# Attention interleaved with a recurrence: a third x buffer, spaced recurrence steps, and two transpositions of each group in scores banks

## What is computed

```python
qkv = x @ c_attn_w + c_attn_b                      # 16 heads of 32
k = concat([cond @ uk_w.T + uk_b, k_word]); v = concat([cond @ uv_w.T + uv_b, v_word])
scores = q @ k.T / sqrt(32), causal (the condition's key is seen by all), + mask
x1 = x + softmax(scores) @ v @ c_proj_w + c_proj_b
h = cond; for t in range(512): h = tanh(h @ Wh + x1[:, t] @ Wx + b)    # 8 rows at once
out = x1 + all h
```

## Time and profile before

| | us |
|---|---|
| median of 3 runs | 1680.48 |
| lowest, highest | 1677.81, 1688.58 |
| profiled execution, its own time | 1685.94 |
| its span from the first to the last instruction | 1684.2 |

### The profile page before, as it was taken

One profiled execution on the slowest core, in us unless ns is written; L12 is line 12 of the kernel. 1 busy time (PEld: TensorE's weight loads), 2 busy tenths in 40 slices (PEclk: granted clock), 3 DMA queues, 4 the chain that ended last, 5 costly groups with the idle time before them and its releaser, 6 DMA issues.

```text
span 1684.2 us, 74145 instructions
## 1 busy us (share of the span) xinstructions
PE 1543.0 (92%) x32749; PEld 1231.0 (73%) x32749; DVE 778.1 (46%) x2687; ACT 667.5 (40%) x2257; POOL 184.5 (11%) x300
## 2 busy tenths in 40 slices
PE   6889989999999999999999999999999989998775
PEld 5667767777777777777777777777778767777554
DVE  4445343544444444544545454454554544565221
ACT  3434333344343433444334443344444434444111
POOL 2112111111110101111010110100101101100000
PEclk8869999999999999999999999999999999999999
DMA  6323121212222222333323232323232432421000
GB/s 229 94 51 86 42 64 49 75 44 75 61 79 78 72 61 71 81 81 86 84 73 91 80 99 83 92 82 96 82 93 70 134 85 70 127 91 42 16 9 15
DMA packets 167903, 130.24 MB, mean 77 GB/s; under 512 B 54264, under 2 KB 153112, under 8 KB 167072
## 3 DMA queue, kind: packets, MB, share of 16 engines
q1 hardware_dynamic: 153792, 92.92, 19.4%
q0 software_dynamic: 13792, 32.58, 6.8%
HBM read 100.00 MB, written 25.43 MB: 74 GB/s over the span
## 4 chain that ended last, share of the span: by engine, by line
PE 81%; DVE 5%; issue 4%; ACT 4%; DMA 3%; SPq 2%; POOL 0%; DVEq 0%; ACTq 0%; POOLq 0%
PE rec L1053 26%; PE dense L983 9%; PE dense L499 9%; PE dense L501 7%; PE dense L500 7%; PE rec L1044 7%; PE scores L975 5%; PE pv L1000 4%; PE pv L1018 2%; PE scores L1053 2%; DMA xin<-x 2%; DVE pre L879 2%; ACT states L732 1%; SPq L524 1%; PE dense L1011 1%
## 5 line engine op out<-in xcount | busy, mean ns | idle before, releaser
L1053 PE MATMUL rec<-wh,states 128*32 128x128 f32 x15360 | 517.7, 275 | 33.6 <-ACT states L732 32.5
L1053 PEld LDWEIGHTS rec<-wh,states 128*32 128x32 f32 x15360 | 401.0, 110 | 119.1 <-ACT states L732 60.3
L879 DVE STREAM_TRANSPOSE pre<-rec 128x128 f32<-128x128 f32 x480 | 152.0, 317 | 515.4 <-PE rec L1053 514.7
L732 ACT ACTIVATE states<-pre 128x32 f32<-128x32 f32 x512 | 133.8, 261 | 510.8 <-DVE pre L879 510.1
L683 ACT ACTIVATE probs<-probs,nmax 128x64 f32<-128x64 f32 (+7 forms) x512 | 271.2, 531 | 103.8 <-DVE nmax L823 100.8
L983 PE MATMUL dense<-ident,probs 128*128 128x128 f32 (+1 forms) x1252 | 229.1, 290 | 31.3 <-DVE probsT L833 8.4
L823 DVE CUSTOM_DVE_ANT_0 probs<-scores,msk,nimg 128x64 f32<-128x64 f32 (+7 forms) x512 | 245.8, 501 | 13.3 <-PE scores L975 6.1
L983 PEld LDWEIGHTS dense<-ident,probs 128*128 128x128 f32 (+1 forms) x1252 | 129.4, 135 | 96.4 <-issue 58.4
L499 PE MATMUL dense<-xT_hi,wqkv_hi 128*128 128x256 f32 x504 | 155.4, 308 | 13.8 <-DVE nimg L809 6.7
L691 ACT COPY probsT<-dense 128x256 f32<-128x256 f32 (+4 forms) x248 | 104.6, 422 | 112.2 <-PE dense L983 111.8
L833 DVE COPY probsT<-dense 128x256 f32<-128x256 f32 (+4 forms) x236 | 119.1, 504 | 59.5 <-PE dense L983 54.7
(11 more groups left out here) (138 smaller groups left out, 1751.4 us busy)
## 6 DMA issues: line engine op xcount, KB each, us to landing
vbuf<-v_dram SPq DMA_DIRECT2D x64, 192.0 KB, 2.8
xin<-x SPq DMA_DIRECT2D x64, 128.0 KB, 2.8
v_dram<-vbuf POOLq DMA_DIRECT2D x64, 128.0 KB, 2.8
out<-outs POOLq DMA_DIRECT2D x32, 256.0 KB, 4.6
vbuf<-v_dram SPq DMA_DIRECT2D x64, 128.0 KB, 2.4
kt<-k_dram SPq DMA_DIRECT2D x16, 512.0 KB, 5.1
vbuf<-v_dram SPq DMA_DIRECT2D x32, 256.0 KB, 3.2
k_dram<-knew POOLq DMA_DIRECT2D x60, 128.0 KB, 2.6
```

The costliest lines, as they stand in the source:

```text
L732: act.activation(state_cells(g), pre[:].rearrange("p f (b z) -> p f b z", z=GROUP)[:, :, :, s], ACT.Tanh).then_inc(h_ready, 1)
L879: dve.transpose(pre_all, rec_bank(g // GROUP)[:, 0:P]).then_inc(pre_ready, 1)
L1053: last = pe.matmul(rec_bank(g // GROUP)[Q * j:Q * j + Q, 0:P], state_tile(g - 1)[:, f, :], wh[:, f, P * j:P * j + P], start=False, stop=f ...
```

## The change

- x has three buffers (XTILES); `xload` of trips 1 and 2 is issued at the start, and `finish(g)` loads trip g + 3 instead of g + 2. SBUF for it comes from the key ring: ROOM goes from 3 to 2 tiles of the longest kind.
- `xsplit` of the next trip goes from head 15 or 16 to 11, and its chunks begin at head 13 instead of 16 or 18.
- In `order`, a step is placed only when at least PACE = 0.7 of weight has been emitted since the step before it.
- The turns of heads with u % 4 in (1, 2) go to `scores[1]` and `scores[2]`, outside the rotation. Such a turn waits for `shifted_ready` of head g + 4, the head whose scores stand in that bank by then; the scores that take the bank next wait for the copy of that turn.
- The `softmax` events of a group are emitted two at the group's first head and one at each of the next two, instead of one, two and one.

```diff
-ROOM = 3 * 2 * S
+ROOM = 2 * 2 * S
-SPLIT_AT = (16, 16, 15, 15, 15, 15, 15, 15)
-CHUNK_AT = (18, 18, 16, 16, 16, 16, 16, 16)
+SPLIT_AT = (11, 11, 11, 11, 11, 11, 11, 11)
+CHUNK_AT = (13, 13, 13, 13, 13, 13, 13, 13)
+XTILES = 3
+PACE = 0.7
...
-        return ([("proj", g, c, 1.5) for c in range(C)] + [("xload", g + 2, 0, 0.0)] * (g + 2 < TRIPS)
+        return ([("proj", g, c, 1.5) for c in range(C)] + [("xload", g + XTILES, 0, 0.0)] * (g + XTILES < TRIPS)
...
-         + chunk(0, 0) + [("vimg", 0, 0, 3.7)] + chunk(0, 1) + chunk(0, 2) + [("xload", 1, 0, 0.0)])
+         + chunk(0, 0) + [("vimg", 0, 0, 3.7)] + chunk(0, 1) + chunk(0, 2) + [("xload", 1, 0, 0.0), ("xload", 2, 0, 0.0)])
...
-            emit([("softmax", v, 0, 0.0) for v in ((u,), (u, u + 1), (u + 1,), ())[u % HC]])
+            emit([("softmax", v, 0, 0.0) for v in ((u, u + 1), (u + 1,), (u + 1,), ())[u % HC]])
...
-    done, t = 0.0, 0
+    done, t, step_at = 0.0, 0, 0.0
...
-               and (done >= whole * (t + 0.5) / FIRST or at + 1 == last)):
+               and (done >= max(whole * (t + 0.5) / FIRST, step_at + PACE) or at + 1 == last)):
             place.setdefault(at, []).append(t)
-            t += 1
+            t, step_at = t + 1, done
...
-        if kind in DENSE_KINDS + ("turn",) and kind != "v":
+        if kind == "turn" and g % HC in (1, 2):
+            n = 2 + g % HC
+            JOB[kind, g, i] = n, uses[n]
+            uses[n] += 1
+        elif kind in DENSE_KINDS + ("turn",) and kind != "v":
...
-        xin = sb("xin", [P, 2, PAIRED, C, P])
+        xin = sb("xin", [P, XTILES, PAIRED, C, P])
...
-        banks = dense + [rec]
+        banks = dense + [rec] + scores[1:3]
...
-                    if g > 1:
-                        wait_copied(sp, "proj", g - 2, C - 2)
-                        wait_copied(sp, "proj", g - 2, C - 1)
+                    if g >= XTILES:
+                        wait_copied(sp, "proj", g - XTILES, C - 2)
+                        wait_copied(sp, "proj", g - XTILES, C - 1)
...
                     if g >= HC:
                         pe.wait_ge(shifted_ready, g - HC + 1)
+                    if j in (1, 2) and group > 1:
+
+                        wait_copied(pe, "turn", g - 2 * HC, 0)
...
                     pe.wait_ge(probs_ready, g + 1)
-                    wait_bank(pe, kind, g, 0)
+                    if g % HC in (1, 2):
+
+                        pe.wait_ge(shifted_ready, min(g + HC + 1, HEADS))
+                    else:
+                        wait_bank(pe, kind, g, 0)
```

More of the change, by code:

```diff
@@ L266, in attention_recurrence @@
     ORDER = order()
-    JOB, DONE, uses, turn, held = {}, {}, [0, 0, 0], 0, None
+    JOB, DONE, uses, turn, held = {}, {}, [0, 0, 0, 0, 0], 0, None
     for kind, g, i in ORDER["PE"]:
-        if kind in DENSE_KINDS + ("turn",) and kind != "v":
+        if kind == "turn" and g % HC in (1, 2):
[3 more added lines that the diff above has]
+        elif kind in DENSE_KINDS + ("turn",) and kind != "v":
             count = 2 if ("xsteps", 0, 0) in JOB else 3
@@ L401, in attention_recurrence @@
         kimg_ready = sem("kimg_ready")
-        x_loaded = [[sem(f"x_loaded{i}_{k}") for k in range(2)] for i in range(2)]
+        x_loaded = [[sem(f"x_loaded{i}_{k}") for k in range(2)] for i in range(XTILES)]
         msk_loaded = [sem(f"msk_loaded{e}") for e in range(2)]
@@ L413, in attention_recurrence @@
         dense_ready = sem("dense_ready")
-        dense_copied = [sem(f"dense_copied{i}") for i in range(3)]
+        dense_copied = [sem(f"dense_copied{i}") for i in range(5)]
         scores_ready = sem("scores_ready")
@@ L523, in load_x @@
                 for pair in range(PAIRED):
-                    eng.dma_start(xin[:, g % 2, pair, 2 * k:2 * k + 2, :].rearrange("p f (e t) -> p (f e) t", e=2),
+                    eng.dma_start(xin[:, g % XTILES, pair, 2 * k:2 * k + 2, :].rearrange("p f (e t) -> p (f e) t", e=2),
                                   x[p // 2 * PAIRS + 2 * r + pair, :, 2 * k:2 * k + 2, :]
                                   .rearrange("p f (e t) -> p (f e) t", e=2)[:, :, W * (p % 2):W * (p % 2) + W]
-                                  ).then_inc(x_loaded[g % 2][k], 16)
+                                  ).then_inc(x_loaded[g % XTILES][k], 16)
         def x_halves(g, k):
-            return xin[:, g % 2, :, 2 * k:2 * k + 2, :].rearrange("p b f t -> p f b t")
+            return xin[:, g % XTILES, :, 2 * k:2 * k + 2, :].rearrange("p b f t -> p f b t")
         def in_pairs(ap):
@@ L669, in _ @@
                 if kind == "xsplit":
-                    act.wait_ge(x_loaded[g % 2][i], 32 * (g // 2 + 1))
+                    act.wait_ge(x_loaded[g % XTILES][i], 32 * (g // XTILES + 1))
                     wait_dense(act, "v", g - 1, 1)
@@ L873, in _ @@
                             scalar=bproj[:, i:i + 1],
-                            in1=xin[:, g % 2, b // 2, i, mine].rearrange("p (m s) -> p m s", s=GROUP),
+                            in1=xin[:, g % XTILES, b // 2, i, mine].rearrange("p (m s) -> p m s", s=GROUP),
                             op0=ALU.add, op1=ALU.add)
```

## The result

| | before | after |
|---|---|---|
| median, us (4 runs each) | 1683.39 | 1712.80 |
| lowest, highest | 1677.81, 1688.58 | 1710.52, 1717.44 |
| profiled execution, its span | 1685.94, 1684.2 | 1710.52, 1708.7 |

The ratio is 1.018, 95% interval 1.0135 to 1.0222: the changed kernel is 29 us slower, where +37 was forecast (1717.5, range 1686 to 1752). In the two profiled executions the span grew by 24.5 us.

A forecast was written before the change was run, and what follows sets the result against it. The prediction took TensorE (busy 92% of the span) to bound the kernel, so its waits decide. Turn waits of +82 and +8 less 53 us removed gave +37 on 1680.48: 1717.5 us, range 1686 to 1752 for 8 times in 10.

The forecast's parts named there:

- What bounds the kernel: TensorE's waits in the 1380 us where attention and steps interleave; its own work stays; at most about 80 us to win.
- The wait of the second turn: Second turn of a group waits for VectorE's softmax of head 4G+1: 66 groups at 1.24 us, +82 us, bounds 60 to 100.
- The third turn: Third turn of a group waits likewise for the softmax of head 4G+2: +8 us, bounds 0 and 25.
- Steps kept apart: Recurrence steps spaced by PACE 0.7, 46 close pairs at about 0.5 us: 22 us removed, bounds 20 and 49.
- x in three buffers: x loaded a trip earlier, so ScalarE's cast no longer waits for it: 13 us removed, bounds 5 and 21.
- The key ring: Two key tiles instead of three, each asked for some five heads ahead: costs nothing, at most 10 us.
- The bank waits: Two turns per group leave the dense banks, so fewer waits for copies out: 18 us removed, bounds 10 and 35.
- The sum: Whole kernel: +82 + 8 - 53 = +37 us, 1717.5 us, 2.2% slower.
- parts 1 to 3: Step spacing, turns leaving the dense banks, and earlier x: together 53 us of TensorE's waits removed, bounds 30 and 90.
- Balance: Rival: turn waits come, but nearly all removable waits go as ScalarE and VectorE catch up: +10, 1690 us; chance 0.17.
- Faster: Rival: the turn's wait is mostly hidden behind TensorE's other work, 40 against 70 us removed: -30, 1650 us; chance 0.08.
- Dearer: Rival: step spacing and third x buffer bring nothing, only 18 us of bank waits return: +72, 1752 us; chance 0.15.

The follow-up runs named there:

- the second experiment: On the kernel before, only the turns of heads 1 and 2 put in scores banks, with the softmax order that goes with it: 1761.4 us, ratio 1.049.

## Why the prediction was right

*What bounds the kernel.* PE's waits ahead of the tail were the right thing to sum: PE's work is the same (32749 matmuls), the tail moved by 0.5 us.

*The wait of the second turn* (+82). The reading of three groups gave 1.19 us each and the planner's rule gave 66 groups. In the changed kernel exactly 66 second turns start 0.15 us behind the end of their softmax, all but one in the groups that the rule named (it missed head 12 of the first trip and named one that did not wait). They give 65 rows with a wait, 79.8 us, 1.23 us each, where 66 times 1.24 was forecast. The 0.05 us in that 1.24, from a release to the matmul, is shown by no run; the runs have 0.15. The three samples of a softmax end in the trace of before were enough, since the order of DVE's list did not change there. The mechanism was then shown from three sides: turns out of these banks (-65 us), softmaxes ahead of the step's transposition (-52), one softmax less (-37).

*The third turn* (+8). 14 third turns wait 4.5 us in all; with the second turn back in the rotation it is 4.5 us in the middle part too. Within its bounds.

*Steps kept apart* (-22). Alone 14 us, mis-sized: the term priced all 46 close pairs by the 1.81 us from step to step, but some waits were a tanh behind the cast of x, and these grew by 6.7 us when the steps moved.

*x in three buffers* (-13). 16 us net, and the ring's loss is in that already; the term was a little low.

*The key ring* (0, at most 10). Wrong by 7.2 us in the changed kernel, within its bound of 10. The step of it that failed is "a tile is asked for some five heads ahead". It holds for a ring in its steady state. Where the tiles' size changes, a tile overlaps the one just before it, and its load may only be issued when the scores of that group are made; it is then asked for one head ahead, behind value loads. In the changed kernel this is so for groups 97 and 113, the two that waited.

*The bank waits* (-18). The three gains of the prediction sum to 53. Between the first step and the tail, 72.8 + 7.2 = 80 us of waits came, and this stretch grew by 22.6 (1393.1 to 1415.7), so 57 went. By the matmul rows the steps' part of that is 18 us (15.5 + 4.8 to 1.1 + 0.8) and the banks' 28 (38 to about 10, the 9 that the prediction gave to x among them, and 3 of the 7.7 behind nimg, which it had left standing). PE's bars there are 6.6 us shorter in all for the same work (1323.4 to 1316.8), which fits the prediction's word that a bar covers part of a wait; some 4 us stay open. The sum of the removed waits was so 4 us too small. For the banks' own term there is a second reading: their waits came to 84.4 us and they cost 65 (62 by the ratios), so 19 to 22 us of other waits went with them, where 18 were forecast.

*The sum.* In the first 165 us, 11.6 us of new waits came and the first step started only 2.1 us later (166.9 against 164.8). The granted clock of this stretch was 0.92 after and 0.84 before, and no run shows that the change made it so: these 9.5 us were in no term and are luck as far as is known. In the profiled executions the +37 thus became +24.5 in this way: second turn 2 less, third turn 4 less, key ring 7 more, removed waits 4 more, start 9.5 less. The errors partly cancel. The bounds 30 and 90 given for parts 1 to 3 are not the sums of the parts' own bounds (20 + 10 + 5 = 35 and 49 + 35 + 21 = 105, or 25 with the ring's 10 us); neither touches the forecast.

*The rivals.* Balance is out by the second experiment. *Faster* named its deciding point rightly: when the second softmax ends soon behind the step. Where a step and no dense product lies between scores and turn (41 groups), the turn waits under 0.5 us in 4 in the changed kernel and in 33 with the softmaxes first; with the banks one lower the turn waits for one softmax less; both kernels are faster than before. *Dearer* is out: spacing and the third x buffer bring 14 and 16 us alone. The rule of the Trainium skill on the drain behind each VectorE instruction (VectorE: DVE Perf Modes, section The DRAIN you can't avoid) would by the prediction's estimate have made the waits 31 us longer. The rows after agree with those before instead: 0.64 us from one softmax to the next at 512 keys (1487.92 to 1488.56), where the first lasts 0.71. The prediction left out what the same section adds, that a next instruction that is not held starts earlier; the rows fit that.

## What to carry to other kernels

A bank that is only lent between two of its users is not a free bank: price it by when its last reader is done, in the reader's own queue, counted from the work that the new user follows in TensorE's order. Before a shared buffer is moved or added, look at what stands ahead of that reader; here the order of the lists of VectorE and ScalarE was worth 52 us, and which two of four banks were lent 37 us. When a ring is made smaller, look at the places where its tiles change size, not at its steady state.

## What the runs showed of the hardware

The granted clock of the first 165 us, where PE has gaps, was 0.84 in the profile of before, 0.92 after, and 0.94 with the turns back in dense banks; the first recurrence step started between 154 and 177 us in the traces of all fourteen kernels. In 11.6 us (84.4 - 72.8) of new waits in that stretch the changed kernel still began its steps only 2 us later than before. A term of a few microseconds in such a stretch is not to be read from one profile.

A second turn starts 0.15 us behind the end of the DVE instruction that releases it, in all 66 places. VectorE starts a softmax of 512 keys 0.64 us after the one before, which lasts 0.71 us, and the softmax behind a transposition of 0.32 us starts 0.24 us after it (1487.68 to 1487.92).
